# Sparse attention stage of a fused network: GpSimd and ScalarE take their work in another order, and the next batch's rows are transposed before the index scores

## What is computed

```python
Q, K, V = jnp.split(x @ w_qkv.T + b_qkv, 3, axis=-1)
Q, K = (_rope(Q), _rope(K))
iq = (x @ w_iq.T + b_iq).reshape(B, S, IDX_HEADS, IDX_DIM)      # 4 heads of 64
ik = x @ w_ik.T + b_ik
iw = x @ w_iw.T + b_iw
head_scores = jax.nn.relu(jnp.einsum('bqhd,bkd->bhqk', iq, ik))
index_scores = jnp.einsum('bhqk,bqh->bqk', head_scores, iw)
_, top_idx = jax.lax.top_k(index_scores, 32)
logits = jnp.einsum('bqd,bkd->bqk', Q, K) * scale + attn_bias   # -inf outside top_idx
attn_out = jnp.einsum('bqk,bkd->bqd', jax.nn.softmax(logits, axis=-1), V)
return attn_out @ w_o.T + b_o
```

## Time and profile before

| | us |
|---|---|
| median of 3 runs (567.18 to 570.19) | 567.39 |
| the profiled execution | 566.95 |
| its span, first to last instruction | 565.1 |
| busy in the span: PE / PEld | 451.0 / 390.7 |
| DVE / ACT / POOL | 380.0 / 337.2 / 288.4 |

### The profile page before, as it was taken

How to read it: one execution, slowest core, us unless ns; L and a number is a source line. 1 busy time by engine, 2 the same in 40 slices (tenths; PEclk the granted TensorE clock), 3 DMA queues, 4 the chain that set the end, 5 groups by cost and what they waited for, 6 DMA issues and landing times. The chain is left out here.

```text
span 565.1 us, 11633 instructions
## 1 busy us (share of the span) xinstructions
PE 451.0 (80%) x3048; PEld 390.7 (69%) x3048; DVE 380.0 (67%) x1501; ACT 337.2 (60%) x934; POOL 288.4 (51%) x329
## 2 busy tenths in 40 slices
PE   1789985859999986999889998889647668786991
PEld 1578865859999874676666766667437568676981
DVE  5789976425666622999999999999957234434661
ACT  1568852226776616889999899998521245434650
POOL 5753440454430025987778777775410633665442
PEclk9989995979999989999999999999756969888996
DMA  8942232131331110011111111110111321121110
GB/s 224 288 135 77 74 90 25 44 88 53 99 87 35 34 34 15 9 37 32 28 30 30 42 44 28 30 30 21 36 35 5 84 57 48 56 64 56 39 36 17
DMA packets 45070, 32.42 MB, mean 57 GB/s; under 512 B 13524, under 2 KB 39508, under 8 KB 45012
## 3 DMA queue, kind: packets, MB, share of 16 engines
q1 hardware_dynamic: 39892, 19.11, 12.2%
q0 software_dynamic: 5120, 12.62, 8.5%
HBM read 19.10 MB, written 12.62 MB: 56 GB/s over the span
## 5 line engine op out<-in xcount | busy, mean ns | idle before, releaser
L629 PE MATMUL bank<-X,w 128*128 x624 | 91.0, 292 | 18.3 <-ACT X L834 16.3
L639 PE MATMUL bank<-WE,hT 128*128 x624 | 89.2, 289 | 14.3 <-ACT hT L847 6.8
L427 POOL DMA_INDIRECT big<-rows,gidx x64 | 61.5, 961 | 74.7 <-DVE gidx L1147 28.2
L629 PEld LDWEIGHTS bank<-X,w 128*128 128x128 f32 x624 | 82.0, 205 | 22.3 <-issue 21.9
L639 PEld LDWEIGHTS bank<-WE,hT 128*128 128x128 f32 x624 | 81.3, 203 | 17.0 <-issue 16.9
L834 ACT ACTIVATE X<-bank 128x128 f32<-128x128 f32 x64 | 17.9, 280 | 94.6 <-PE bank L620 60.9
L1179 DVE TENSOR_SCALAR hT<-bank,w 128x128 f32<-128x128 f32 x156 | 47.6, 346 | 39.0 <-issue 12.2
L660 PE MATMUL bank<-xbT,WB 128*128 128x256 f32 x224 | 59.2, 394 | 13.2 <-ACT xbT L872 8.5
L839 ACT ACTIVATE w<-WE 128x644 f32 x78 | 57.5, 738 | 3.1 <-DVE big L1191 2.8
L847 ACT ACTIVATE hT<-bank,w 128x128 f32<-128x128 f32 x156 | 48.7, 367 | 13.4 <-PE bank L629 10.1
L447 POOL DMA_INDIRECT X<-x,pidx x32 | 31.7, 989 | 48.7 <-DMA x<-big 41.2
(11 more groups left out here) (161 smaller groups left out, 1026.6 us busy)
## 6 DMA issues: line engine op xcount, KB each, us to landing
WE<-w_experts SPq DMA_DIRECT2D x2, 2048.0 KB, 11.5
rows<-xf SPq DMA_DIRECT2D x32, 128.0 KB, 2.2
rows<-X SPq DMA_DIRECT2D x32, 128.0 KB, 2.7
X<-x SPq DMA_DIRECT2D x4, 512.0 KB, 7.6
x<-big SPq DMA_DIRECT2D x32, 64.0 KB, 1.5
big<-rows,gidx POOLq DMA_INDIRECT x64
WB<-w_idx SPq DMA_DIRECT2D x1, 640.0 KB, 5.7
WE<-b SPq DMA_DIRECT2D x1, 512.0 KB, 12.9
```

Of the source, the lines that this page charges most:

```text
L427: pool.indirect_dma_start(xg[:, j, :], None, rows_dram[n], bass.IndirectOffsetOnAxis(ap=gidx[:, j:j + 1], axis=0)).then_inc(f["g"][j % G_R ...
L629: mm = pe.matmul(bank[r + 2 * (k // 2)][:, k % 2 * P:(k % 2 + 1) * P], w1[st.slot(1, 4)][:, k * P:(k + 1) * P], moving, start=True, stop=True)
L639: mm = pe.matmul(bank[4 + r][:, 0:D], hT[r][:, k, :], WE[:, bass.ds(expert[(s - 2) % TURN], 1), W2_AT + k * D:W2_AT + (k + 1) * D].rearran ...
```

## The change

Four edits in the sparse attention, and one in the experts:

1. GpSimd's step begins with `gather_x(s + 3)`, `inverse_std(s - 1)` and the bias; then come the three rotary operations, and only then both `add_heads`.
2. TensorE transposes the rows of batch s + 1 (`turn_rows`) in step s, between the product with the values and the index scores of half 0, into bank 4 instead of bank 5.
3. ScalarE copies them (`turned`) after `part` of half 0, ahead of `xf_out` and of the ReLU of half 1.
4. ScalarE copies the values out (`projected(3, (1,))`) after `iw` and `normalise_b`, where it stood ahead of them.
5. `opens` is false beyond step 32, so VectorE's load of registers in step 40 of each expert stage is gone.

```diff
         def opens(st, lag):
-            return (st.base - HEAD) % TURN == 0 or st.base == lag or st.base == T
+            return st.base <= T and ((st.base - HEAD) % TURN == 0 or st.base == lag or st.base == T)
...
             for s in range(B + 2):                                  # GpSimd
                 b, r = s, s % 2
+                if b + 3 < B:
+                    gather_x(b + 3)
+                if s > 0:
+                    inverse_std(s - 1)
                 if b < B:
+                    pool.wait_ge(b_["xb"], b + 1)
+                    pool.tensor_tensor(X[...], X[...], bo_bc[...], ALU.add).then_inc(b_["xo"], 1)
                     pool.wait_ge(b_["pje"], 8 * b + 7)
                     pool.tensor_tensor(qk[r][:, 0:2, :], ..., const("cos")..., ALU.mult)
                     pool.tensor_tensor(qk[r][:, 2:4, :], ..., const("sin")..., ALU.mult)
-                    add_heads(b, r, 0)
                     pool.wait_ge(b_["rp"], 2 * (b + 1))
                     after(pool, b_["S"], C * (b - 1))
                     pool.tensor_tensor(qr[r][:, :, :], ..., ALU.add).then_inc(b_["qr"], 1)
+                    add_heads(b, r, 0)
                     add_heads(b, r, 1)
-                inverse_std(s)
-                if b < B:
-                    ... the bias ...
-                if b + 3 < B:
-                    gather_x(b + 3)
+            inverse_std(B + 1)
...
+            def turn_rows(b, r):                                    # TensorE
+                pe.wait_ge(b_["xb"], b + 1)
+                for c in range(C):
+                    mm = pe.transpose(bank[4][:, c * P:(c + 1) * P], xb[r][:, c, :], ident)
+                mm.then_inc(b_["T"], 1)
+            turn_rows(0, 0)
...
-                if st.on(0, B):
-                    pe.wait_ge(b_["xb"], b + 1)
-                    after(pe, b_["iwe"], b)
-                    after(pe, tails[1]["xfT"], b - 3)
-                    ... transposes into bank[5] ...
...
                 if st.on(2, B):
                     ... probabilities times values ...
+                if st.on(-1, B):
+                    turn_rows(st.item(-1), st.slot(-1, 2))
                 if st.on(0, B):
                     index_scores(0)
...
                 if st.on(0, B):                                     # ScalarE
-                    projected(3)
+                    projected(3, (0,))
                     ... iw ...
                 if st.on(-1, B):
                     normalise_b(st, -1)
+                if st.on(0, B):
+                    projected(3, (1,))
                 for c in range(C):
                     ... rel ...
-                    if c == C - 1 and st.on(-1, B):
-                        turned(st.item(-1), st.slot(-1, 2))
                     ... part ...
+                    if c == 0 and st.on(-1, B):
+                        turned(st.item(-1), st.slot(-1, 2))
                     if c == 0 and st.on(3, B):
                         xf_out(1, st.item(3), st.slot(3, 2), bank[5][:, 0:S])
```

More of the change, by code:

```diff
@@ L478, in _ @@
                 b, r = s, s % 2
+                if b + 3 < B:
+                    gather_x(b + 3)
+                if s > 0:
+                    inverse_std(s - 1)
                 if b < B:
+                    pool.wait_ge(b_["xb"], b + 1)
+                    pool.tensor_tensor(X[:, b * C:(b + 1) * C, :], X[:, b * C:(b + 1) * C, :],
+                                       bo_bc[:, :].unsqueeze(1).to_broadcast([P, C, D]), ALU.add).then_inc(b_["xo"], 1)
                     pool.wait_ge(b_["pje"], 8 * b + 7)
@@ L488, in _ @@
                     pool.tensor_tensor(qr[r][:, :, :], qk[r][:, 0:2, :], qk[r][:, 2:4, :], ALU.add).then_inc(b_["qr"], 1)
+                    add_heads(b, r, 0)
                     add_heads(b, r, 1)
-                inverse_std(s)
-                if b < B:
-                    pool.wait_ge(b_["xb"], b + 1)
-                    pool.tensor_tensor(X[:, b * C:(b + 1) * C, :], X[:, b * C:(b + 1) * C, :],
-                                       bo_bc[:, :].unsqueeze(1).to_broadcast([P, C, D]), ALU.add).then_inc(b_["xo"], 1)
-                if b + 3 < B:
-                    gather_x(b + 3)
+            inverse_std(B + 1)
             experts_pool(1)
@@ L683, in index_scores @@
                             mm.then_inc(b_["idx"], 1)
-                if st.on(0, B):
-                    b, r = st.item(0), st.slot(0, 2)
-                    pe.wait_ge(b_["xb"], b + 1)
-                    after(pe, b_["iwe"], b)
-                    after(pe, tails[1]["xfT"], b - 3)
-                    for c in range(C):
-                        mm = pe.transpose(bank[5][:, c * P:(c + 1) * P], xb[r][:, c, :], ident)
-                    mm.then_inc(b_["T"], 1)
                 if st.on(4, B):
@@ L711, in _ @@
                     b, r = st.item(0), st.slot(0, 2)
+                    after(pe, tails[1]["xfT"], b - 3)
                     pe.matmul(bank[5][:, S:S + C * IDX_HEADS], ones[0:1, :], rowc[:, 0:C * IDX_HEADS], start=True, stop=False)
@@ L871, in turned @@
                 after(act, b_["idx"], 2 * C * (b - 1))
-                act.activation(xbT[r][:, :], bank[5][:, 0:S], ACT.Copy).then_inc(b_["xbT"], 1)
+                act.activation(xbT[r][:, :], bank[4][:, 0:S], ACT.Copy).then_inc(b_["xbT"], 1)
             normalise_b(Step(0), 0)
@@ L877, in _, with projected @@
                 b, r = st.item(0), st.slot(0, 2)
-                def projected(pair):
+                def projected(pair, which=(0, 1)):
                     act.wait_ge(b_["pj"], 5 * b + pair + 1)
-                    for i in (2 * pair, 2 * pair + 1):
+                    for i in (2 * pair + w for w in which):
                         src = bank[2 + pair % 2][:, i % 2 * S:(i % 2 + 1) * S]
```

## The result

The changed kernel takes **628.2 us** (median of 4 runs, 623.7 to 630.5), the kernel before 567.3 beside it: 1.105 times as long, interval 1.098 to 1.113. I had forecast 578.5. The profiled execution of the changed kernel took 630.54 us, 63.6 more than that of before.

A forecast was written before the change was run, and what follows sets the result against it. Bound: a loop through ScalarE and TensorE, 11.84 us a step. A new loop of 12.83 us a turn made the stage +14.2, the loads gave -3.1: 578.05 from 566.95, adjusted to the median 578.5 us, range 571 to 585.

The forecast's parts named there:

- The bound: Sparse stage before the change: a loop through ScalarE and TensorE sets the pace, 11.84 us a step in the steady middle.
- the older loop: Sparse stage, the loop without GpSimd: lengthens to 12.3 us a step and decides where the new loop is shorter.
- The loads: Ends of both expert stages: without VectorE's TENSOR_LOAD, 1.56 us less each, -3.1 in all.
- A lock: VectorE's `xf_b` scaling beside GpSimd's L493: 0.39 us longer, in a path of 1.17 from `rs` to `xb`.
- It did not exist before: The new 12.83 us loop through all engines: claimed absent before, because index scores did not wait for the next batch's `xb`.
- The held gather: GpSimd's gather beside VectorE's two-input SBUF operations: at most 1.4 us a turn over ten turns, 592 us; chance 0.05.
- The rival of a gain: ScalarE's freed wait ahead of `vb` shortens a turn to 11.1 us; 555 us with the loads; chance 0.08.

The follow-up runs named there:

- one exchange in GpSimd's order: The changed kernel with `inverse_std` moved back ahead of the gather in GpSimd's step: 577.4 us against 567.9 for the kernel before, ratio 1.019.
- the run with TensorE's clock kept up: The changed kernel with 11 useless unit-matrix transposes on TensorE ahead of its wait for the next batch's rows: 608.3 us against 569.9 for the kernel before.
- GpSimd's order alone: The kernel before with only GpSimd's new order (edit 1): 574.1 us against 567.9, ratio 1.013.
- values later: The kernel before with the register loads gone and `vb` copied behind the normalised rows (edits 5 and 4): ratio 0.996 to the kernel before.
- the kernel with the holding taken away: The changed kernel with GpSimd's bias waiting for `nb`, until the shift is done: 583.6 us against 569.9 for the kernel before, ratio 1.020.
- edit 5 alone: The kernel before with only the new `opens` (no register load in step 40 of the expert stages): 563.9 us against 567.9, ratio 0.995.

## Why the prediction was wrong

- **The bound, the older loop, the direction: right.** TensorE's and ScalarE's edits without GpSimd's give 12.36 a step (12.3 forecast). The forecast mechanism, `rs` late by the gather and ScalarE, TensorE and ReLU waiting for it one after another, is what the waits show, and one exchange in GpSimd's order takes it away.
- **The loads: right at one end.** VectorE follows TensorE 1.57 sooner at both ends (1.56 forecast), but at the first the profiled executions give most of it back to TensorE's lower clock; the sum had 3.1, the traces show 1.6.
- **The step that failed first: "A lock", sized 0.39.** I let L493 hold the first scaling and took the second scaling and the shift at their free durations. With the new order GpSimd has three more operations ready, the bias, the cosines and the sines, without a gap, and each of VectorE's three operations ends with one of them: 3.21 from `rs` to `xb` in place of 1.17, 2.0 a turn. The rows for it were in my groups: two durations (0.97 for a pair beside one sum) tell what one GpSimd operation costs, and the order before the prediction tells how many follow it. With it the turn would have been 14.9; the run with TensorE's clock kept up measured 15.1.
- **The second: TensorE's clock was not in the sum.** I wrote that the first index scores wait for `xb`, and did not ask what TensorE's standing does to TensorE: 2.75 us ahead of the transposes, then the lower level through scores and logits, 2.1 a turn by experiment. It also makes the first two steps 13.7 and 15.4 to 15.5 long in three of the kernels, where they are 12.0 and 13.0 with the clock kept up. Steps 1 to 3 took 45.1 against 36.1 forecast, and 40.5 with the clock kept up, so 4.6 of those 9.0 are the clock.
- **The sum with both** is 12.83 + 2.0 + 2.1 = 16.9 a turn against 17.2; the last 0.3 stay open. Over steps 4 to 12 that is 46 of the 48 us lost there, of which I had forecast 8.6.
- **"It did not exist before" was wrong in its reason.** The loop ran through ScalarE's order before, with 2.1 us of slack: GpSimd's order alone costs 1.3%. The transposes ahead of the scores put 1.5 us more in it.
- **The rivals.** The held gather was a good question with a small answer: the first DMA takes 1.28 beside VectorE's additions where it took 1.04. The rival of a gain falls by the run with the values later: scores are as late as ScalarE is. My range had no case in which GpSimd holds VectorE more than once.

The Trainium skill (SBUF — State Buffer, "SBUF: two separate sides") says that VectorE and GpSimd share one pair of ports under an exclusive lock: a VectorE operation with two inputs in SBUF (as the shift has) or in one of its faster two-port modes, and a GpSimd operation that reads SBUF, do not run together; whoever starts first has the pair for its whole instruction. The trace agrees, with 1.23 us for a shift of two columns. The same page's figure for a gather beside a VectorE copy ("A bandwidth-pool intuition that's wrong"), weighed in the prediction, is for such a two-port mode, and the additions that the gather met here are operations with two inputs; they cost it 0.24 us, and no run here has the other case.

## What to carry to other kernels

Write down the loop that an order closes, engine by engine, before counting what an edit frees: an engine with slack (GpSimd, 76% busy here) is no reason to put something ahead of the one value that another engine waits for. Where one engine's operations were seen to hold another's, count for each waiting operation the next operation in line on the other engine, not one in all. And a new wait on TensorE has to be priced twice if the clock falls behind it, as the wait and as the work at half the clock: here it fell behind 2.75 us of standing once a step.

## What the runs showed of the hardware that was not expected

- A VectorE instruction on 128x2 values took 1.23 us instead of 0.15 beside a GpSimd product of 1.25 us: the cost of being held does not depend on how small the held operation is.
- Two such streams alternate: three VectorE operations in a row (3.11 us where they take 0.77 in the earlier trace rows) were held by three GpSimd operations in a row, each ending 0.02 to 0.09 us behind its one, and GpSimd lost nothing (its products took 1.25 each, 1.27 in the kernel with the holding taken away).
- Adding a wait to GpSimd and adding useless work to TensorE each made the changed kernel faster, by 45 and by 20 us.
- The stages around the sparse one took different times on two chips, in two kernels that do not differ there: from the last batch's first addition to the end 134.6 us (values later) and 163.8 (edit 5 alone), and to the first addition 215.1 and 225.6, with the steady steps equal (11.86). The cause is open.
